# One product per token for values, mask and gates, with gates taken bank by bank

## What is computed

```python
m = mask[..., None]
zn = _layernorm(z, ln_in_w, ln_in_b)
a = m * jax.nn.sigmoid(jnp.einsum('bijc,hc->bijh', zn, a_g_w) + a_g_b) * (jnp.einsum('bijc,hc->bijh', zn, a_p_w) + a_p_b)
b = m * jax.nn.sigmoid(jnp.einsum('bijc,hc->bijh', zn, b_g_w) + b_g_b) * (jnp.einsum('bijc,hc->bijh', zn, b_p_w) + b_p_b)
x = jnp.einsum('bikh,bjkh->bijh', a, b)
xn = _layernorm(x, ln_out_w, ln_out_b)
gate = jax.nn.sigmoid(jnp.einsum('bijc,oc->bijo', zn, g_w) + g_b)
out = gate * (jnp.einsum('bijh,oh->bijo', xn, z_w) + z_b)
```

## Time and profile before

| | |
|---|---|
| time, median of 3 runs | 302.03 us (301.5 to 302.27) |
| the profiled execution's own time | 302.3 us |
| its span in the trace | 300.5 us |
| busy, share of the span | PE 82%, DVE 74%, ACT 73%, POOL 43% |
| mean granted TensorE clock, share of full speed | 0.898 |
| the projection stage in that span | 243.8 us (first L1218) to 266.6 us (first L1240) |

### The profile page before, as it was taken

The page is one execution under the profiler, slowest core; times in us unless marked ns, Lnnn a source line. Parts: engine busy times, 40 slices in busy tenths (PEclk is TensorE's granted clock), DMA queues, the critical chain, the costliest instruction groups (busy, mean ns, idle before and its releaser), DMA issues.

```text
span 300.5 us, 7271 instructions
## 1 busy us (share of the span) xinstructions
PE 247.1 (82%) x2394; PEld 196.3 (65%) x2394; DVE 223.4 (74%) x512; ACT 219.9 (73%) x980; POOL 129.3 (43%) x143
## 2 busy tenths in 40 slices
PE   0687670999999999999999999999847699859840
PEld 0677320767787878787877787878637566558840
DVE  3088951789998888889888888998643738968790
ACT  1545660799988999999989999989662645559590
POOL 5940000245454455454454545455400007999172
PEclk9999595699999999999999999999985969975695
DMA  9200045254434353534434354320000000000028
GB/s 144 39 10 2 8 134 166 99 200 163 146 123 165 123 194 135 189 121 151 159 109 164 139 194 143 114 106 4 2 0 0 0 2 2 0 2 0 0 36 123
DMA packets 42312, 27.13 MB, mean 90 GB/s; under 512 B 24324, under 2 KB 42276, under 8 KB 42276
## 3 DMA queue, kind: packets, MB, share of 16 engines
q1 hardware_dynamic: 36572, 25.95, 27.1%
q10 hardware_dynamic: 5704, 0.72, 1.6%
HBM read 1.38 MB, written 1.18 MB: 9 GB/s over the span
## 4 chain that ended last, share of the span: by engine, by line
PE 70%; DVE 12%; ACT 6%; DMA 3%; SPq 3%; issue 2%; POOL 2%; POOLq 1%; DVEq 0%; ACTq 0%
PE psum L1181 11%; PE psum L1129 11%; PE psum L1192 10%; PE psum L1130 5%; PE psum L1132 5%; PE psum L1161 5%; PE psum L1046 4%; PE psum L1149 2%; PE psum L1024 2%; PE psum L1067 2%; PE psum L1169 2%; PE psum L1109 2%; DVE shared L993 2%; DMA maps<-in_x 2%; PE psum L1218 2%
## 5 line engine op out<-in xcount | busy, mean ns | idle before, releaser
L506 POOL TENSOR_TENSOR probs<-probs,rden 96x384 f32<-96x384 f32 x96 | 79.1, 824 | 119.1 <-DVE rden L960 119.1
L659 ACT ACTIVATE probs<-psum,neg_max 96x96 f32<-96x96 f32 x384 | 124.5, 351 | 2.5 <-PE psum L1181 0.5
L659 ACT ACTIVATION_READ_ACCUMULATOR probs<-psum,neg_max 96x1 f32 x384 | 83.2, 217 | 0.0
L954 DVE COPY probs_t<-psum 96x384 f32<-96x384 f32 x96 | 52.9, 551 | 20.1 <-PE psum L1181 18.8
L923 DVE TENSOR_REDUCE neg_max<-psum 96x4 f32<-96x384 f32 x96 | 50.9, 530 | 1.4 <-PE psum L1132 1.4
L1181 PE MATMUL psum<-ident,probs 96*96 96x96 f32 x384 | 47.7, 246 | 1.1 <-DVE probs_t L954 0.9
L1129 PE MATMUL psum<-u_st,x_stack 128*96 128x384 f32 x96 | 40.8, 425 | 8.6 <-DVE bias_lo L914 8.2
L1181 PEld LDWEIGHTS psum<-ident,probs 96*96 96x96 f32 x384 | 37.6, 125 | 5.5 <-issue 1.4
L1192 PE MATMUL psum<-probs_t,v_sb 128*32 128x96 f32 x768 | 35.8, 258 | 0.0
L1130 PE MATMUL psum<-bias_hi,ident_r 128*96 128x384 f32 x96 | 33.3, 347 | 0.0
L1132 PE MATMUL psum<-bias_lo,ident_r 128*96 128x384 f32 x96 | 33.1, 345 | 0.0
(11 more groups left out here) (172 smaller groups left out, 434.3 us busy)
## 6 DMA issues: line engine op xcount, KB each, us to landing
u_st<-u_split SPq DMA_DIRECT2D x96, 192.0 KB
x_stack<-shared SPq DMA_DIRECT2D x40, 96.0 KB, 2.0
maps<-in_x SPq DMA_DIRECT2D x4, 288.0 KB, 5.0
x_stack<-shared SPq DMA_DIRECT2D x4, 144.0 KB, 2.1
out_y<-maps SPq DMA_DIRECT2D x6, 96.0 KB, 3.1
out_y<-maps ACTq DMA_DIRECT2D x6, 96.0 KB, 3.5
bias_lo<-gate_sb SPq DMA_DIRECT2D x24, 12.0 KB
x_stack<-shared SPq DMA_DIRECT2D x4, 48.0 KB, 1.9
```

What stands on the lines that cost most here:

```text
L506: pool.tensor_tensor(probs[:, m % SLOTS], probs[:, m % SLOTS], rden[:, m, :].unsqueeze(2).to_broadcast([N, H, N]), ALU.mult).then_inc(prob ...
L659: e = act.activation(probs[:, m % SLOTS, h], bank_s[m % 4][0:N, h * N:(h + 1) * N], ACT.Exp, bias=neg_max[:, m, h:h + 1], accum_out=den[:, ...
L954: dve.tensor_copy(probs_t[0:N, (m - T_BEHIND) % 2].rearrange("p h q -> p (h q)"), bank_t[0:N, 0:H * N]).then_inc(t_ready, 1)
```

## The change

The masked values and their three tiles go, with the semaphore `values_masked` and the function `mask_values`. ACT starts on a set as soon as it is projected and takes the gates bank by bank: for each member f the 192 a and b gates, then the 96 output gates, eight operations a set. `gates_ready` counts eight a set (GATE_READS). DVE waits for both gates of a bank and then does three operations, one for each block: `scalar_tensor_tensor` takes 64 values from PSUM, multiplies them with a [96, 1] column of the mask (`mask1_t[:, i:i + 1]`) and with the 64 gates, and writes the token row's 64 numbers of `ab`. After the twelfth it signals `ab_ready`. PE waits for `ab_ready` of the set before the last, where it waited for its gates.

```diff
-MASKED = 3
+GATE_READS = 2 * GROUP
...
-                pool.wait_ge(gates_ready, 2 * n + 2)
+                pool.wait_ge(gates_ready, GATE_READS * (n + 1))
...
             for n in range(SETS):
-                act.wait_ge(values_masked, n + 1)
+                act.wait_ge(proj_done, n + 1)
                 need(act, ab_ready, n - 1)
-                act.activation(gates_ab[:, n % 2], projections(n, slice(0, VALUES * C)), ACT.Sigmoid).then_inc(gates_ready, 1)
-                act.activation(gate_sb[:, trio(n)].rearrange("j b f c -> j f b c"),
-                               projections(n, slice(VALUES * C, GATES * C)), ACT.Sigmoid).then_inc(gates_ready, 1)
+                for f in range(GROUP):
+                    act.activation(gates_ab[:, n % 2, f], projections(n, slice(0, VALUES * C))[:, f],
+                                   ACT.Sigmoid).then_inc(gates_ready, 1)
+                    act.activation(gate_sb[:, trio(n), f], projections(n, slice(VALUES * C, GATES * C))[:, f],
+                                   ACT.Sigmoid).then_inc(gates_ready, 1)
...
-            mask_rows = mask1_t[:, :].rearrange("p (f b) -> p f b", f=GROUP)
-
-            def mask_values(n):
-
-                dve.wait_ge(proj_done, n + 1)
-                need(dve, ab_ready, n + 1 - MASKED)
-                dve.tensor_tensor(masked[n % MASKED], projections(n, slice(GATES * C, PW)),
-                                  mask_rows[:, :, trio(n)].unsqueeze(3).to_broadcast([N, GROUP, TRIO, VALUES * C]),
-                                  ALU.mult).then_inc(values_masked, 1)
-
-            mask_values(0)
             for n in range(SETS):
-                if n + 1 < SETS:
-                    mask_values(n + 1)
-                dve.wait_ge(values_masked, n + 1)
-                dve.wait_ge(gates_ready, 2 * n + 1)
-                dve.tensor_tensor(ab.rearrange("k (f b) t h -> k f b (t h)", f=GROUP)[:, :, trio(n)],
-                                  masked[n % MASKED], gates_ab[:, n % 2], ALU.mult).then_inc(ab_ready, 1)
+                for f in range(GROUP):
+                    dve.wait_ge(gates_ready, GATE_READS * n + 2 * f + 2)
+                    for t in range(TRIO):
+                        i = f * BLOCKS + TRIO * n + t
+                        product = dve.scalar_tensor_tensor(
+                            ab[:, i].rearrange("k t h -> k (t h)"), projections(n, slice(GATES * C, PW))[:, f, t],
+                            mask1_t[:, i:i + 1], gates_ab[:, n % 2, f, t], ALU.mult, ALU.mult)
+                product.then_inc(ab_ready, 1)
...
-                need(pe, gates_ready, 2 * (n - 1))
+                need(pe, ab_ready, n - 1)
...
-            pe.wait_ge(gates_ready, 2 * SETS)
+            pe.wait_ge(gates_ready, GATE_READS * SETS)
             pe.wait_ge(ab_ready, SETS)
```

More of the change, by code:

```diff
@@ L129, in triangle_kernel @@
         tok = sb("tok", [N, 4, BLOCKS, GROUP])
-        masked_more = sb("masked_more", [N, H * HD * 3 // 2])
         u_split = sb("u_split", [P, 2, 2, GN], f32r)
@@ L189, in triangle_kernel @@
             "p (b n) -> p b n", n=N)
-        masked = [v.rearrange("j (f b c) -> j f b c", f=GROUP, b=TRIO)
-                  for v in (masked_more[:, :], probs_t[0:N].rearrange("j s h q -> j (s h q)"),
-                            o_sb[0:N].rearrange("j s f n -> j (s f n)"))]
         gates_ab = probs.rearrange("j s h k -> j (s h k)").rearrange("j (s f b c) -> j s f b c", s=2, f=GROUP, b=TRIO)
@@ L246, in triangle_kernel @@
         tri_stack_copied = sem("tri_stack_copied")
-        values_masked = sem("values_masked")
         deviated = sem("deviated")
```

## The result

The changed kernel takes 305.19 us (median of 12 runs), the kernel before 302.80 over as many beside it: a ratio of 1.0074, 95% interval 1.0052 to 1.0097, or some 2.2 us slower. The profiled execution after took 304.64 us, its span is 302.8 us against 300.5. The forecast was 302.6, +0.6 on the 302.03 then known. So the side was right, and the size was about a quarter of what came.

A forecast was written before the change was run, and what follows sets the result against it. DVE was taken to bound the projection stage; its last product at 256.24 + 60 x 0.18 = 267.04 us, 0.59 later than 266.45, carried to the end unchanged, gave a median of 302.6 us on 302.03, range 299.9 to 304.6.

The forecast's parts named there:

- The bound: In the projection stage ahead of the triangle product, DVE, busy 16.45 of 17.23 us, bounds the steady part.
- the ring: In the projection stage, two sets cycle through release, projection, first gate and products: 5.0 us against 4.5 now.
- d: Start-to-start interval of one 64-element mask product on DVE, taken as 0.18 us, bounds 0.11 to 0.214.
- the formula: End of the stage's last product: 256.24 + 60d, so 267.04 us, 0.59 later than 266.45; break-even at d = 0.170.
- The pointer: Reading the mask column through a pointer adds 0.05 to 0.08 us to each DVE product's interval.
- The base: Fixed part of a DVE product without a pointer, beyond 0.067 us for 64 elements: 0.04 to 0.07 us.
- the pointer is dear: At DVE's issue of the next product, d is 0.185 to 0.23; at 0.214, 2.6 us later, 304.6 us; 33%.
- the forecast case: In the projection stage, d from 0.155 to 0.185 with the clock falling as now: 301.1 to 302.9 us; 42%.
- Behind the stage all moves along: From the triangle product to the end, everything shifts by the projection stage's 0.59 us.
- PE keeps its clock: At the triangle product PE stays at full clock: three banks take 2.1 us, not 4.22; time 300.5 us; 8%.
- The covers: Costed at nothing: ACT's 1.5 us a set hidden behind DVE's 2.16, POOL done by 268.6, ACT's table change within 2.7 us.
- A collision of pointer and POOL: In DVE's products, pointer reads collide with POOL: d 0.25 or more, +5 us, 307 us; 5%.

The follow-up runs named there:

- bank release run: Changed kernel, DVE signalling after each bank's three products and PE waiting for that bank alone: ratio 1.0008 to the kernel before.
- run with a constant: Changed kernel with constant 1.0 in place of the mask column read through a pointer, mask left out: ratio 0.9977 to the kernel before.
- run with the filled pause: Changed kernel with four bias matmuls in PE's pause between triangle product and transposes: ratio 0.9947 to the kernel before, a second time 0.9965.
- run with the finer gates alone: Kernel before with only ACT's gates taken bank by bank, eight operations a set, mask products kept: ratio 1.0071 to the kernel before.
- run with the filled wait: Changed kernel with eight bias matmuls into a free bank in PE's wait ahead of the triangle product: ratio 1.006 to the kernel before.

## Why the prediction was wrong, and where it was right

**The bound and the ring were right.** DVE bounds the stage, the ring is release, projection, first gate, twelve products, and each of its parts came as priced: 0.05, 2.2, 0.50 for a forecast 0.51, and a ring of 5.13, where 2.75 + 12 x 0.192 + 0.085 is 5.14. With the measured d the formula gives 256.24 + 60 x 0.192 = 267.76 for the last product, 1.31 later than 266.45; the stage grew by 1.24. The bank release run confirms the ring's part, 1.48 us, and the run with a constant the pointer's: without either of them the loss is gone.

**The step that failed is the price of d.** I took 0.18 and got 0.192: sixty times 0.012 is 0.72 us, which turns the forecast 0.59 into 1.31 where the stage lost 1.24. That is all that was missing in the stage, and somewhat less than half of what was missing in all. The pointer was right, 0.060 for an expected 0.05 to 0.08. The base was not: 0.132 - 0.067 = 0.065 without a pointer, while I allowed 0.04 to 0.07 and then moved the value "a little lower for the PSUM base". The row behind 0.04 was one pair of different operations (L966 to L923 in the earlier trace rows); the row L828 to L831, with 0.07, was the nearer. Base 0.065 to 0.07 plus pointer 0.06 would have given 0.19 to 0.20. The Trainium skill's ("Vector Engine (DVE) Microarchitecture Reference", 5.2) fixed 75 ns for an instruction, with which I had an estimated 0.142, fits the pointer-free run better than the 0.04 did; it has no term for the pointer, and the measured d is 0.05 above it. (The L810 row that I set beside it shows four starts, not six.)

**The rival "the pointer is dear" is where it landed.** Its range began at 0.185 and its place, DVE's issue of the next product, is the right one; its end of 0.214 was too high. I gave it 33% and the forecast case 42%, though both rested on the same three L750 rows.

**"Behind the stage all moves along" was wrong.** I carried 0.59 to the end unchanged. Behind the stage 0.14 + 0.5 us were added. In the triangle part it is DVE's sum, here one bank's in the chain of before and one of after:

```profile
272.77 0.68 DVE probs L859
```

```profile
274.48 0.73 DVE probs L856
```

L856 lasts 0.73 to 0.86 in the chain where L859 was 0.68 to 0.75 (POOL is at work beside both; why it is more in after wasn't tried). In the output part it is the clock, which returned 20.5 us after its fall in place of 17.1. This was nowhere in the forecast: the rows on the clock that I read ended at 268, while the return at 284 decides how fast the output begins. It isn't a plain function of the stage's length either: with the constant the stage took only 20.93 us, and the output part 17.83 as in after, while with the banks released one by one (22.60) it took 17.36.

**The rival "PE keeps its clock" had a false price.** 4.22 us would not have become 2.1, since those matmuls go at one pace at either clock. What the run with the filled pause showed in its place is that the clock is worth 1.9 us at the transposes and 0.9 in the output part.

**The covers held.** ACT stays hidden, but the forecast gave as reason only that 1.5 us a set is less than 2.16. The run with the finer gates alone points to a second condition, that ACT starts at the projection: behind the mask product the same eight operations are on the path. POOL ends early and brings nothing, as said. A collision of pointer and POOL didn't come.

**The range.** 299.9 to 304.6 stood on a median of 302.03; over the twelve runs beside after, the kernel before has 302.80, 0.77 more. Against its own median the range's upper end is +2.6 us and the change is +2.2 to +2.4, inside; in absolute time 305.19 lies outside. Three runs fixed the median less well than the 0.3% that I used for "no change".

## What to carry to other kernels

Price many small operations by their interval, and take the fixed part from a pair of the same operation: a product of 64 elements is two thirds fixed cost here, and half of that is the pointer. When a consumer that was off the ring becomes the one that frees a buffer, write down the ring and put its slowest hand-over into the sum; release in pieces (here a bank) takes it off again. Follow a forecast past the stage to every place where the clock, or another state, is still to change.

## What the runs showed of the hardware

- A [96, 1] pointer as the scalar of a fused DVE product of 96x64, one input in PSUM, adds 0.060 us to the interval (0.192 against 0.132) and 63 ns to the duration (273 against 210).
- The triangle product's 96x96 fp32 matmuls go at the same pace at both clocks, 0.18 us each at 1.00 (16 in 2.90 us) and 0.17 at 0.50 (64 in 10.74), while the transposes behind them speed up: 24 in 4.10 us at 1.2 GHz and in 2.20 at 2.4. At 2.4 GHz a weight load lasts 238 to 258 ns in the former and 140 in the latter. The triangle product takes every 64th number of a row of `ab`, the transposes whole runs; that this is the reason is an argument only, and wasn't tried.
- The granted clock fell while PE was busy without a gap (271.9 us in the run with the filled wait), and through 10.74 us of gapless triangle product it did not come back. In fourteen profiles it then stayed at 0.50 for 13.7, 17.1 or 20.5 us and no other time; a fill of PE's pause went with the shortest in one kernel, twice, and with the middle one in the profiled executions of two near relatives.
